# A decoder layer on one core: products stored by halves of the channels, and four pieces placed elsewhere in their slots

## The reference

```python
x = layernorm(x + mamba(x));  x = layernorm(x + attention(x, ctx));  x = layernorm(x + experts(x))

def mamba(x):                       # d_inner 512, 16 states, chunks of 64 tokens
    xc, res = split(x @ W_in.T + b_in)
    u = silu(depthwise_conv3(xc) + conv_b)
    dlt, B, C = split(u @ W_x.T)
    delta = softplus(dlt @ W_dt.T + b_dt)
    dA = exp(delta * A);  dBu = delta * B * u          # per channel and state
    h[t] = dA[t] * h[t-1] + dBu[t]                      # restarts at each chunk
    y = sum over states of h * C
    return (y * silu(res)) @ W_out.T + b_out

def attention(q_in, kv):            # 16 heads of 16
    q, k, v = projections; out = softmax(q k^T / 4) v; return out @ w_o.T + b_o

def experts(x): return (silu(x @ w1) * (x @ w3)) @ w2   # 8 experts, 704 wide
```

## Time and profile before

| | |
|---|---|
| median of 3 runs | 2794.8 us |
| profiled execution | 2790.39 us, span 2788.5 us |
| PE | 2425.0 us busy (87%) |
| DVE | 2148.2 us busy (77%) |
| POOL | 2008.2 us busy (72%) |
| ACT | 1840.4 us busy (66%) |
| first phase | about the first 2200 us, in steps of about 67 us |
| DMA | 399.63 MB, mean 143 GB/s |

### The profile page before, as it was taken

The page is one execution under the profiler, slowest core; times in us unless marked ns, Lnnn a source line. Parts: engine busy times, 40 slices in busy tenths (PEclk is TensorE's granted clock), DMA queues, the critical chain, the costliest instruction groups (busy, mean ns, idle before and its releaser), DMA issues. The chain is left out here.

```text
span 2788.5 us, 49586 instructions
## 1 busy us (share of the span) xinstructions
PE 2425.0 (87%) x14816; PEld 1668.8 (60%) x14816; DVE 2148.2 (77%) x3262; ACT 1840.4 (66%) x4007; POOL 2008.2 (72%) x1000
## 2 busy tenths in 40 slices
PE   5678888899888889888989889898897869999998
PEld 3356666666666666666666666666665545555554
DVE  2788999999999999999999999999999732322332
ACT  3667888888888888888888878888887541111111
POOL 4998999999999999999999999999999400000000
PEclk9888999999999999999999999999999879999999
DMA  4465666666666676666666666666666360343221
GB/s 145 116 141 150 155 163 168 160 161 158 158 158 159 165 166 169 158 165 166 164 168 162 165 161 163 174 166 162 172 161 154 86 181 12 92 129 93 78 79 31
DMA packets 319321, 399.63 MB, mean 143 GB/s; under 512 B 115697, under 2 KB 256241, under 8 KB 314962
## 3 DMA queue, kind: packets, MB, share of 16 engines
q1 hardware_dynamic: 303698, 384.91, 53.9%
q10 hardware_dynamic: 15360, 11.55, 1.5%
HBM read 300.86 MB, written 94.37 MB: 142 GB/s over the span
## 5 line engine op out<-in xcount | busy, mean ns | idle before, releaser
L515 POOL TENSOR_TENSOR arena<-arena 128x1024 f32<-128x1024 f32 x512 | 1208.6, 2364 | 77.5 <-DMA arena<-w_dram 67.1
L615 ACT ACTIVATE dA_ps<-arena,a_neg 128x256 f32<-128x256 f32 x2048 | 880.1, 465 | 253.4 <-DVE arena L812 110.8
L799 DVE TENSOR_TENSOR_SCAN arena<-dA_ps,arena 128x512 f32<-128x512 f32 x608 | 728.1, 1207 | 85.2 <-ACT dA_ps L615 75.4
L525 POOL TENSOR_TENSOR arena<-arena 128x512 f32<-128x512 f32 (+1 forms) x416 | 739.1, 1777 | 61.8 <-DVE arena L799 58.7
L799 DVE TENSOR_TENSOR_SCAN dA_ps<-dA_ps,arena 128x512 f32<-128x512 f32 x416 | 493.2, 1205 | 3.1 <-POOL arena L515 2.7
L906 PE MATMUL a_ps<-xT,w_conv 128*128 128x256 f32 x1536 | 367.0, 389 | 0.0
L856 DVE TENSOR_REDUCE mx<-s_ps 128x2 f32<-128x512 f32 x497 | 334.5, 673 | 24.0 <-PE s_ps L906 23.9
L677 ACT ACTIVATE probs<-st_ps 128x512 f32<-128x512 f32 x493 | 285.5, 579 | 54.2 <-PE st_ps L906 46.5
L906 PEld LDWEIGHTS a_ps<-xT,w_conv 128*128 128x128 f32 x1536 | 286.8, 193 | 53.3 <-issue 16.5
L906 PE MATMUL s_ps<-k_st,q_st 96*128 96x256 f32 x994 | 266.6, 351 | 51.9 <-DVE mx L856 39.4
L906 PE MATMUL y_ps<-arena,sel 128*32 128x256 f32 x4096 | 257.7, 394 | 50.5 <-DVE m_rows L862 27.1
(11 more groups left out here) (112 smaller groups left out, 3268.0 us busy)
## 6 DMA issues: line engine op xcount, KB each, us to landing
arena<-delta_dram SPq DMA_DIRECT2D x512, 128.0 KB, 2.8
arena<-w_dram SPq DMA_DIRECT2D x512, 128.0 KB, 3.3
arena<-bc_dram SPq DMA_DIRECT2D x128, 256.0 KB, 4.5
q_st<-q_parts_dram SPq DMA_DIRECT2D x512, 64.0 KB
k_st<-k_parts_dram SPq DMA_DIRECT2D x512, 64.0 KB
w_dram<-u SPq DMA_DIRECT2D x32, 512.0 KB, 2.9
delta_dram<-delta SPq DMA_DIRECT2D x32, 512.0 KB, 3.8
k_parts_dram<-parts SPq DMA_DIRECT2D x32, 512.0 KB, 4.0
```

Of the source, the lines that this page charges most:

```text
L515: pool.tensor_tensor(dBu[:, n % NB], w_r[:, n // RP % 2, t % RP].unsqueeze(1).to_broadcast([P, QS, L]), bc_r[:, b.par, 0], ALU.mult).then_ ...
L525: pool.tensor_tensor(h[:, n % NH, states], h[:, n % NH, states], bc_r[:, b.par, 1, states], ALU.mult).then_inc(s_hC, 1)
L615: last = nc.scalar.activation(dA[n % NDA][:, q], delta_r[:, n // (2 * RP) % 2, t % RP], ACT.Exp, scale=a_neg[:, t, 2 * half + q:2 * half + ...
L799: nc.vector.tensor_tensor_scan(dst, decays, dBu[:, n % NB, 2 * half:2 * half + 2].rearrange("p q t -> p (q t)"), 0.0, ALU.mult, ALU.add).t ...
```

## The change

It has four edits.

1. w and delta are formed, cut and stored in two halves of two channel blocks each. POOL runs a product of 128x512 and a cut of 128x8 twice, and SP stores w and delta of a half each, with semaphores of their own per half. The channels are permuted in the weights (`spread`), and the DRAM tensors are laid out by blocks, so that `replicate(0)` and `replicate(1)` need only the first half, `replicate(2)` and `replicate(3)` only the second. ACT waits by halves too (`conv_evac`).
2. On SP `replicate(0)` moves from near the end to the head of the list: in slot 14 it stands ahead of the store of q, where it stood behind it.
3. On ACT the high part of the second group's maxima (`max_high(1)`) moves ahead of `silu` in slot 9.
4. On DVE the first residual and the head norms move behind the scans of the second half.

```diff
-            def delta_store(b):
-                wait_all(sp, (s_cut, 1, b, 1), *[(s, 128, b.back(2), 128) for s in s_rep])
-                sp.dma_start(d_dram[b.par], delta[:].rearrange("p k t -> p (k t)")).then_inc(s_d_st, 16)
-            def w_store(b):
-                wait_all(sp, (s_w, 1, b, 1), *[(s, 128, b.back(2), 128) for s in s_rep])
-                sp.dma_start(w_dram[b.par], u[:].rearrange("p k t -> p (k t)")).then_inc(s_w_st, 16)
+            def store_half(half):
+                def piece(b):
+                    blocks = slice(2 * half, 2 * half + 2)
+                    wait_all(sp, (s_w, 2, b, half + 1), *[(s, 128, b.back(2), 128) for s in s_rep])
+                    sp.dma_start(w_dram[b.par, blocks].rearrange("k p t -> p k t"), u[:, blocks]).then_inc(s_w_st[half], 16)
+                    wait_all(sp, (s_cut, 2, b, half + 1))
+                    sp.dma_start(d_dram[b.par, blocks].rearrange("k p t -> p k t"),
+                                 delta[:, blocks]).then_inc(s_d_st[half], 16)
+                return piece
             def replicate(part):
-                    wait_all(sp, (s_d_st, 16, b, 16), (s_w_st, 16, b, 16))
+                    wait_all(sp, (s_d_st[part // 2], 16, b, 16), (s_w_st[part // 2], 16, b, 16))
...
             run_steps([                                   # SP
+                (O_REP + 1, replicate(0)),
                 (O_K - 2, load_ctx),
                 (O_Q + 3, store_parts(q_dram, s_q_hi, s_q_lo, s_q_dram)),
...
-                (O_SP + 2, w_store),
-                (O_SP + 2, delta_store),
+                *[(O_SP + 2, store_half(half)) for half in range(2)],
                 (O_XP + 2, bc_load),
-                (O_REP + 1, replicate(0)),
...
-            def w_piece(b):                               # POOL
-                pool.wait_ge(s_delta, b.value(2, 2))
-                pool.tensor_tensor(u[:], u[:], delta[:], ALU.mult).then_inc(s_w, 1)
+            def w_piece(half):
+                def piece(b):
+                    blocks = slice(2 * half, 2 * half + 2)
+                    pool.wait_ge(s_delta, b.value(2, half + 1))
+                    pool.wait_ge(s_xp_mm, b.value(1, 1))
+                    pool.tensor_tensor(u[:, blocks], u[:, blocks], delta[:, blocks], ALU.mult).then_inc(s_w, 1)
+                    pool.wait_ge(s_w, b.value(2, half + 1))
+                    starts = delta[:, blocks].rearrange("p k (c t) -> p k c t", t=CH)[:, :, :, 0:1]
+                    nc.gpsimd.memset(starts, CUT).then_inc(s_cut, 1)
...
             run_steps([                                   # ACT
                 (O_V + 1, v_evac),
+                (O_MT + HG + 1, max_high(1)),
                 (O_SILU, silu),
...
-                *[(O_MT + HG * gr + 1, max_high(gr)) for gr in range(NG)],
+                *[(O_MT + HG * gr + 1, max_high(gr)) for gr in range(NG) if gr != 1],
...
             run_steps([                                   # DVE
+                *[(O_SCAN + t, scan(t, 1)) for t in range(NU)],
                 (O_OUT + 1, residual(0, s_out_mm, a_ps, s_r1, s_st1, s_mv1, s_ln1, s_xtok, 16)),
                 *[(O_ON + HG * gr + 1, head_norm(gr)) for gr in range(NG)],
-                *[(O_SCAN + t, scan(t, 1)) for t in range(NU)],
...
-    spread = (CT * (4 * (part % 4) + block) + part // 4).reshape(-1)
+    spread = (CT * (4 * block + part % 4) + part // 4).reshape(-1)
```

More of the change, by code:

```diff
@@ L292, in mixers @@
         s_dt_mm, s_delta, s_w = sem("dt_proj_done"), sem("delta_ready"), sem("w_ready")
-        s_cut, s_d_st, s_w_st = sem("delta_cut_at_chunks"), sem("delta_in_dram"), sem("w_in_dram")
+        s_cut, s_d_st, s_w_st = sem("delta_cut_at_chunks"), *(
+            [sem(f"{n}_half_{i}_in_dram") for i in range(2)] for n in ("delta", "w"))
         s_rep = [sem(f"delta_w_replicated_{i}") for i in range(NU // 4)]
@@ L381, in piece @@
                     n = b.value(NU // RP, part)
-                    cols = slice(RP * L * part, RP * L * (part + 1))
-                    wait_all(sp, (s_d_st, 16, b, 16), (s_w_st, 16, b, 16))
+                    wait_all(sp, (s_d_st[part // 2], 16, b, 16), (s_w_st[part // 2], 16, b, 16))
                     if n >= 2:
@@ L388, in piece @@
                     for tile, dram in ((delta_r, d_dram), (w_r, w_dram)):
-                        src = dram[b.par].rearrange("(i s) c -> i (s c)", s=4)[:, cols]
+                        src = dram[b.par, part].rearrange("(i s) t -> i (s t)", s=4)
                         for j in range(4):
@@ L484, in _ @@
             sp.wait_ge(s_m_dram, 16 * B * NG)
-            sp.wait_ge(s_d_st, 16 * B)
-            sp.wait_ge(s_w_st, 16 * B)
+            for half in range(2):
+                sp.wait_ge(s_d_st[half], 16 * B)
+                sp.wait_ge(s_w_st[half], 16 * B)
             sp.wait_ge(s_bc_st, 16 * B)
@@ L498, in _ @@
             pool.wait_ge(s_const_v, N_SET)
-            def w_piece(b):
-                pool.wait_ge(s_delta, b.value(2, 2))
-                pool.wait_ge(s_xp_mm, b.value(1, 1))
-                pool.tensor_tensor(u[:], u[:], delta[:], ALU.mult).then_inc(s_w, 1)
-                pool.wait_ge(s_w, b.value(1, 1))
-                starts = delta[:].rearrange("p k (c t) -> p k c t", t=CH)[:, :, :, 0:1]
-                nc.gpsimd.memset(starts, CUT).then_inc(s_cut, 1)
+            def w_piece(half):
[7 more added lines that the diff above has]
+                    nc.gpsimd.memset(starts, CUT).then_inc(s_cut, 1)
+                return piece
             def dBu_piece(t):
@@ L530, in _ @@
                 *[(O_SCAN + t - 1, dBu_piece(t)) for t in range(NU)],
-                (O_SP + 2, w_piece),
+                *[(O_SP + 2, w_piece(half)) for half in range(2)],
                 *[(O_SCAN + t + 1, hC_piece(t)) for t in HC_POOL],
@@ L547, in piece @@
                     if b.back(1):
-                        act.wait_ge(s_w_st, b.back(1).value(16, 16))
+                        act.wait_ge(s_w_st[half], b.back(1).value(16, 16))
                     nc.scalar.activation(u[:, 2 * half:2 * half + 2], a_ps[:], ACT.Copy).then_inc(s_conv, 1)
@@ L595, in softplus @@
                 if b.back(1):
-                    act.wait_ge(s_w, b.back(1).value(1, 1))
-                    act.wait_ge(s_d_st, b.back(1).value(16, 16))
+                    act.wait_ge(s_w, b.back(1).value(2, 2))
+                    for half in range(2):
+                        act.wait_ge(s_d_st[half], b.back(1).value(16, 16))
                 for half, ps in enumerate((a_ps, f_ps)):
@@ L1386, in decoder_layer @@
     m_dram = nc.dram_tensor("max_rows_dram", (NG, 2, HG * L), F32, kind="Internal").ap()
-    d_dram = nc.dram_tensor("delta_dram", (2, P, ND * L), F32, kind="Internal").ap()
-    w_dram = nc.dram_tensor("w_dram", (2, P, ND * L), F32, kind="Internal").ap()
+    d_dram = nc.dram_tensor("delta_dram", (2, ND, P, L), F32, kind="Internal").ap()
+    w_dram = nc.dram_tensor("w_dram", (2, ND, P, L), F32, kind="Internal").ap()
     bc_dram = nc.dram_tensor("bc_dram", (2, 2 * NS, L), F32, kind="Internal").ap()
```

## The result

| | before | after |
|---|---|---|
| median | 2794.53 us (4 runs) | 2879.82 us (4 runs) |
| lowest and highest | 2786.76, 2800.88 | 2869.76, 2887.82 |
| profiled execution | 2790.39 us | 2869.76 us |

The ratio is 1.0305 [1.0283, 1.0327]: the change costs 85 us, or 2.84 us in each of the 30 steps in which `replicate(0)` and the store of q meet. 2895 us was forecast, 3.5 us per step.

What follows compares the result with a forecast made beforehand. A closed chain over several engines, 67.24 us, was taken to bound the step. Terms 2.6 + 0.8 - 1.3 + 0.6 + 0.8 = +3.5 us in 30 steps, +105 us on 2790.39, gave 2895 us, range 2850 to 2945.

Steps and rivals of the forecast that it cites:

- closed chain: scores(0) on PE to silu on ACT, w on POOL, load_ctx on SP, back to scores(0): 67.24 us, the step.
- No slack: Claim that the closed chain has no spare time in the step read; PE waited 0.58 us for load_stack(0)'s last DMA.
- The order in slot 14: On SP, the store of q's landing is no longer hidden under replicate(0)'s issue: +2.6 us per step (0.9 to 5.7).
- The clock: On PE, the wait at scores(0) lowers the clock for the conv matmuls behind it: +0.8 us per step (0 to 2.6).
- What catches up: Behind scores(0), DVE's waits for POOL's product and the residual's input are given back: -1.3 us per step (0 to -1.3).
- max_high(1): On ACT, the copy ahead of silu waits for PE's transpose and delays silu: +0.6 us per step (0 to +1.0).
- The head norms: In slot 12, a scan ahead of DVE's head norm delays v_proj and load_ctx: +0.8 us per step (0 to +1.2).
- The halves: POOL starts sooner, but replicate(0) still waits behind load_ctx on SP: 0 us per step (-0.6 to +0.5).
- Rival A: Faster: PE's spare time at scores(0) hides SP's wait; about -1.1 us per step, 2756 us; chance 0.17.
- B: No change: store latency mostly hidden, clock stays, 2790 us, chance 0.08; weak form 2800 to 2850 us, chance 0.07.
- C: Much slower: load_stack(1) and replicate(1) move too, POOL and w are late; +5.5 us per step, 2955 us; chance 0.08.
- D: The change doesn't do what it says; expected for the halves, with no time and no chance of its own.

Runs made afterwards that it cites:

- e2: The kernel before with one edit, replicate(0) ahead of the store of q on SP: 2851.55 us, ratio 1.0205 to before.
- e1: The changed kernel with replicate(0) put back behind the store of q, other edits kept: 2801.84 us, ratio 1.0015 to before.
- e4: The changed kernel with max_high(1) put back behind silu on ACT: 2885.04 us, ratio 1.0318 to before.
- e3: The changed kernel with the four head norms back ahead of the second scans, first residual still behind them: 2859.04 us, ratio 1.0215 to before.
- e5: The kernel before with the halves alone, all else in its old place: 2792.84 us, ratio 0.9989 to before.
- e10: The changed kernel with replicate(0), max_high(1) and the last head norm in their old places: 2789.32 us, ratio 0.9977 to before.
- e9: The changed kernel with replicate(1) a slot sooner on SP, ahead of load_stack(1): 2890.03 us, ratio 1.0322 to before.

## Why the prediction was right

The sum was 3.5 us per step, and 2.84 were measured. The closed chain of the forecast can be read again in after, link by link (SP and PE rows above; `silu` begins at 1128.57, in the rows of ACT below). Beside it stand the means over 28 steps, read from the same rows of every step, and those of the two runs that do or undo the order in slot 14 alone.

| link | step read, before | step read, after | mean before | mean e2 | mean e1 | mean after |
|---|---|---|---|---|---|---|
| `load_ctx` to scores(0) | 13.66 | 15.32 | 14.31 | 15.68 | 13.58 | 15.23 |
| scores(0) to `silu` | 33.38 | 34.74 | 33.88 | 34.54 | 33.75 | 34.55 |
| `silu` to w | 12.33 | 11.69 | 12.33 | 12.33 | 11.70 | 11.70 |
| w to `load_ctx` | 7.87 | 8.01 | 6.95 | 6.75 | 9.08 | 8.80 |
| sum | 67.24 | 69.76 | 67.47 | 69.31 | 68.11 | 70.28 |

Three things in my reading of this chain were wrong, though the forecast survived them. The sum equals the step for any four events that each step holds once, so it did not show that the chain binds; only the waits can. "No slack" held for the step read, but in 25 of the 28 steps of before PE did not wait for `load_stack(0)` at scores(0) at all; in after it waits there in all 28, for 51 us together. And w is only a mark in time: in both steps read PE waits for ACT's delta ahead of q_proj, and goes on from there to `v_proj` and `load_ctx` without POOL. A w that starts sooner, as with the halves, shortens one link and lengthens the next.

**The order in slot 14**, forecast +2.6, measured +1.65 (e1 to after, first link; +1.37 from before to e2). This is the mechanism, and e1 and e2 show that it is. From e1 to after the first read goes out 3.2 us later behind `load_ctx` (8.89 instead of 5.72 us in the mean), where I had 3.5. The landing of the store of q is now 4.3 us in the median, against 3.9 taken. What I had too small is what comes back behind it: 0.4 us in the issue of the nine DMAs (3.73 instead of 4.17 us) and 1.1 between the last of them and scores(0) (2.51 instead of 3.66). I had allowed 0.9 for both. The step read of before and after also gives +1.66, but there the store's 3.92 us came back as 1.26 in issue and 1.0 behind it, and that agreement is chance: between the means of before and after the link grows by 0.92 only, since the other edits shorten it by 0.73 (before to e1).

**The clock**, forecast +0.8. From e1 to after scores(0) to `silu` grows by 0.80 in the mean. The group of all conv matmuls agrees, in after and in before:

```profile
L912 PE MATMUL a_ps<-xT,w_conv 128*128 128x256 f32 x1536 | 391.4, 408 | 0.0
```

```profile
L906 PE MATMUL a_ps<-xT,w_conv 128*128 128x256 f32 x1536 | 367.0, 389 | 0.0
```

The mean goes from 389 to 408 ns, 24.4 us in all, which is 0.8 per step. The twelve conv matmuls behind scores(0) took over 3.5 us in at least 11 of the 28 steps of after, and in one of before. All of PE is 34 us longer busy, 1.1 per step, and e1 with the old order takes 29 of these back (2430.2 us busy). That conv's longer work is lost time one for one is argued from the link; no run holds the clock and moves the order.

**What catches up**, forecast -1.3, did not come. Of the two waits of DVE, that for the residual's input is still there (0.59 us in the step read of after, 38.7 us in all instead of 40.6), in spite of the scan ahead of it. And DVE now waits longer for PE's scores. DVE in the step read:

```profile
1100.68 0.69 DVE L862 TENSOR_REDUCE mx<-s_ps 128x2 f32<-128x512 f32 x1 [1.03 <-PE s_ps L912]
...
1105.57 0.69 DVE L862 TENSOR_REDUCE mx<-s_ps 128x2 f32<-128x512 f32 x1 [1.95 <-PE s_ps L912]
...
1131.05 0.27 DVE L868 SCALAR_TENSOR_TENSOR m_rows<-y_ps,m_rows 8x128 fp32r<-8x128 f32 x1
1134.08 1.22 DVE L805 TENSOR_TENSOR_SCAN arena<-dA_ps,arena 128x512 f32<-128x512 f32 x1 [2.76 <-ACT dA_ps L620]
```

I had PE late, and still gave back what only counts where DVE is late. That was an inconsistency in my own sum. The sign that belonged to it failed too: I expected POOL's wait for w to be smaller, and it grew from 67 to 161 us.

**`max_high(1)`**, forecast +0.6, is 0 with the new order. ACT in the step read:

```profile
1128.30 0.25 ACT L720 ACTIVATE m_rows<-y_ps 8x128 fp32r<-8x128 f32 x1
1128.57 1.28 ACT L570 ACT_TABLE_LOAD   x1
```

There is no wait ahead of the copy, since PE's transpose started at 1127.76, 0.8 us ahead of `silu`, where it started 0.2 after it before. The copy takes about 0.3 us of ACT, which e4 cannot see. The half of the step that was right is DVE: it gains nothing from the earlier copy, and waits 2.76 us for the decay instead (before, 2.14 for the high part).

**The head norms**, forecast +0.8 or 24 us, measured 21 us with the order changed (e3). From the means of e3 to those of after, w to `load_ctx` grows from 7.41 to 8.80; the two links behind it fall by 1.1 together between these two profiled executions, and e3's was the slowest of its four, so what the norms cost stands on the medians. In the step read that link grew by 0.14 only, and there two things met: before was read in a step whose `v_proj` ran at half clock (3.40 us, one of 11 such steps of 32), after in one at full clock (1.99 us). The next step of after reads 9.19 from w to `load_ctx`, with the matmuls at 3.17.

**The halves**, forecast 0, are 0 (e5). w does start 0.6 us sooner, and nothing follows from it, since the condition that ends last for `replicate(0)` is `load_ctx`, as forecast. By an estimate from the Trainium skill, "DMA: Bandwidth & Descriptors", section "Anatomy of one DMA — SWDGE (gpsimd) path", a half would land some 0.6 us ahead of the whole; here the halves of delta take 3.8 us in the median, as the whole did, and the halves of w 3.6 us where the whole took 2.9.

**The terms do not add.** The order alone costs 57 us, the other three without it 4, all together 85. The 4 is itself a difference: e10, which takes the last head norm and `max_high(1)` back, is 11 us faster than e1 and 6 faster than before. So these two places cost some 11 us with the old order too, and what stays of the halves, the residual and the other norms gives 6 back; neither the residual nor the other norms were tried by themselves. The means show where the rest of the delay goes with the old order. From before to e1 the stretch from `silu` to `load_ctx` grows by 1.5 us, and the next link, up to scores(0), shrinks by 0.7, while PE waits there in 17 of 28 steps instead of 3: PE had time to spare, and `load_ctx` came late into it. With the new order that spare time is already spent. The remaining links fall by 0.1, and the profiled e1 (2809.17 us) was the slowest of its runs.

So the mechanism of the forecast is right and was shown, and that the total came within 0.7 us per step is in part luck: the order was nearly 1.0 and `max_high(1)` 0.6 too high, and the 1.3 that I gave back did not come.

Rival A fell with PE's wait at scores(0), B with e1 and e2, C with e9, as far as that run goes. D held for the halves. My range for eight in ten, 2785 to 2945, held chances of 0.75 by my own list.

## What to carry to other kernels

In a queue that issues in order, a DMA is also a piece of time, and may be what hides the landing of the store ahead of it. Before moving it, look at what then stands right behind the store, and put there what nobody waits for; what others need soon goes first. A wait that vanishes from the profile is a gain only if the chain through it is the one that closes the step. To find that chain, follow who waits for whom over many steps: that its links add up to the step's length says nothing, as they always do. Then price each edit by its link, in the mean of all steps, since one step can differ from another by several us.

## What the runs showed of the hardware that I had not expected

- Steps with nearly the same waits got different clocks. In after PE stood still for 1.33 and then 1.91 us in the step read, the clock fell to 0.50 behind it and conv took 4.31 us, with the clock back at 0.96 before its end; in the next step it stood still for 1.19 and then 2.12 us, and conv took 2.86:

```profile
1164.78 0.51 PE L912 MATMUL s_ps<-k_st,q_st 96*128 96x256 f32 x2 [2.12 <-DMA q_st<-k_st]
...
1166.87 2.86 PE L912 MATMUL a_ps<-xT,w_conv 128*128 128x256 f32 x12
```

  In after the low stretch falls now on `v_proj` (18 steps of 32), now on conv. Such a price is read from the group's mean over all steps, not from one.
- Behind a stretch in which SP issued nothing for some 4 us, the DMAs that followed were issued and landed faster: 0.4 us less for the issue of the nine, and 1.1 us less from the last of them to scores(0) (means of after against e1). In the step read it was 1.26 and 1.0.
- Stores of delta of 512 and of 256 KB land alike (3.8 us in the median); those of w took 2.9 us whole and 3.6 us by halves.
